# One decoder layer on one core: second and third norm folded, x1 transposed before its norm, the batch loop written out

## The chip, the cores and the metric

The kernel runs on 1 core of one Trainium2 chip. The time is the device time of one execution in microseconds (us); lower is better. The core has engines with one instruction queue each: PE (matmuls), DVE (VectorE), ACT (ScalarE), POOL (GpSimd) and SP, which only issues transfers. Each runs its queue in order; they wait for one another on semaphores.

## What is computed

Four sequences (B = 4) of T = 256 rows, D = 256 columns, in f32. Cut to what matters:

```
h  = layernorm(x);  q,k,v = h@Wq, h@Wk, h@Wv; rotary on q,k
x1 = x + rms_norm(lightning_attention(q,k,v)) @ Wo     # 16 heads of 16, chunks of 128, a decay per head
kv  = ctx @ W_k.T + b_k                                 # 256 x 64
sim = (layernorm(x1) @ kv) @ kv.T / 16                  # 256 x 256
z   = (sim - mean(sim)) * rsqrt(var(sim) + 1e-6) * gamma + beta
x2  = x1 + softmax(z)
h3  = layernorm(x2); logits = h3 @ Wr; gate = softmax of the two largest of 8
out = x2 + sum_e gate[e] * (h3 @ We[e] + be[e])
```

Note for the change that a row of softmax(z) sums to 1, so its mean is 1/256.

## The kernel before, in words

Each sequence is two tiles of 128 rows (t = 0, 1). The work of a sequence has three stages: **front** (norm 1, q/k/v, rotary, attention, x1), **back** (norm 2, context product, similarities, softmax, x2, norm 3, routing) and **experts** (8 units, u = 0 to 7; a unit is one tile times two experts, six f32r matmuls of 512 columns, a high and low part product, into one bank of 2 KB per partition). Passes are skewed: pass i does the front of sequence i, the back of sequence i-1 and the experts of sequence i-2. Pass 0 has a front only, pass 1 front and back, passes 2 and 3 all three (these two are called the full passes here), pass 4 back and experts, pass 5 experts only. Passes 2 and 3 are one hardware loop (L263).

The order on each queue is written out by hand in one `body(i, front, back, experts)` per engine. `late(steady=..., last=...)` marks where the expert work of the older sequence goes: on PE the units (`expert_unit`), on DVE the additions (`add_units(b, q)`: four additions, n = 4q to 4q+3, two for each of the units 2q and 2q+1, in the order tile 0, tile 1, tile 0, tile 1). A unit that reuses a bank waits on PE for the additions that read it (`s_exd`). Eight banks: `bank[0..5]` for everything, `ebank[0..1]` for the experts. In a full pass the units 2 and 3 go to bank2 and bank3, the others alternate between the two ebanks.

What the prediction's steps touch, in a full pass:

- PE: `qkv(t)` is the q/k product (L784, 512 columns) followed by the v product (256 columns) into `bank[2 + t]`. For t = 1 that is bank3, which also holds the similarities of tile 0, so `qkv(1)` waits for `s_z` of both tiles between its two products. Then the transposes of q and k (L961), `scores`, the transposes of x2 (L799), `attend`, `project`.
- ACT: copies out of PSUM. `normalize_similarities` (L411) writes `z` and increments `s_z`; `head_queries` (kT L423, qx L425) follows the q/k transposes, then the second `softmax_exp` (ez L417).
- DVE: norm statistics (`ln_stats`: stats L519, mv L522, ve L524), `ln_apply` (norm L530), additions (L557), `softmax_input` (zg L592, zb L594, nmax L598), `rotate` (L584, L587), `residual2` (rsum L604, x2 L606), `decay_scores` (probs L613), `route` (gates, L621 to L654), x1 (L767).
- POOL: every rsqrt as a power (L325), the addition of the experts' biases to `acc` once 12 additions are done (L336), the sine half of the rotary (rot_b L346), the decayed keys (L352).
- `keep_clock(n, bank)` (L792) issues n matmuls that nobody reads.

Of the kernel before, what the change touches and what calls it, by code (L numbers as in the profile page):

```python
# [100 lines left out]
def decoder_layer(nc, x, ctx, wq, wk, wv, wo, rms_w, w_k, b_k, ln_gamma, ln_beta, wr, we, be,  # L101
                  consts, decay, out):
    with ExitStack() as stack:
# [211 lines left out]
        def _(pool):  # L315
# [11 lines left out]
            def body(i, front, back, experts):  # L327
                if back:
                    rsqrt(rs[1], ve[1], i - 1, s_var[1], s_rstd[1])
                if front:  # L330
# [719 lines left out]
```

## Time and profile before

| | |
|---|---|
| time, median of 3 runs (lowest to highest) | 180.23 us (179.91 to 180.83) |
| profiled execution: span from first to last instruction | 178.7 us |
| profiled execution: its own time | not given apart from the span; the median lies 1.5 us above the span |
| PE busy | 152.3 us (85%) |
| DVE busy | 126.4 us (71%) |
| ACT busy | 61.8 us (35%) |
| POOL busy | 35.9 us (20%) |
| mean granted TensorE clock | 0.971 of full speed |
| DMA over the span | 7.29 MB, mean 41 GB/s |

Busy time counts instructions of an engine; PE's matmuls are pipelined and their ends are modelled. "Idle before" names the time an engine stood idle just before a row, and "<-" what ended that idle time. A granted clock of 1.00 is 2.4 GHz and 0.50 is 1.2 GHz.

### The profile page before, as it was taken

What the parts mean: (1) busy time and instruction counts of PE and PEld (TensorE: products, weight loads), DVE (VectorE), ACT (ScalarE), POOL (GpSimd) and SP (SyncE); (2) the same over time, 40 slices, a digit from 0 to 9 for tenths busy, and PEclk for the clock granted to TensorE, in tenths of its full rate; (3) what the DMA queues carried; (4) which work ended last, traced back from release to release, by engine and by line L of the source; (5) the groups of instructions that cost most, each with busy time, mean ns of one, the idle gap of its engine ahead of it and who ended that gap; (6) DMA issues with size and microseconds to landing.
All of it is one profiled execution on the core that took longest, in us unless ns stands there. A gap on an engine that the chain in (4) does not pass through costs nothing.

```text
span 178.7 us, 3036 instructions
## 1 busy us (share of the span) xinstructions
PE 152.3 (85%) x983; PEld 106.6 (60%) x983; DVE 126.4 (71%) x396; ACT 61.8 (35%) x171; POOL 35.9 (20%) x54
## 2 busy tenths in 40 slices
PE   0399964797997999999959999999599889998991
PEld 0267433573662678867626888677258757745880
DVE  0633599647487995975789959757899565877762
ACT  3346880103487132054751320547613220311110
POOL 3104163013161002222410013125100113010020
PEclk9999996569999999999999999999999999999999
DMA  5999200000200000000004000000010000001001
GB/s 173 290 360 340 57 0 4 0 0 2 69 10 0 0 4 0 0 2 0 0 4 132 0 0 0 0 0 0 0 59 0 4 2 0 0 0 59 4 0 59
DMA packets 7930, 7.29 MB, mean 41 GB/s; under 512 B 2264, under 2 KB 7664, under 8 KB 7792
## 3 DMA queue, kind: packets, MB, share of 16 engines
q1 hardware_dynamic: 7424, 6.79, 12.1%
q10 hardware_dynamic: 496, 0.37, 0.7%
q8 instruction: 6, 0.10, 0.2%
q14 instruction: 4, 0.03, 0.1%
HBM read 6.11 MB, written 1.05 MB: 40 GB/s over the span
## 4 chain that ended last, share of the span: by engine, by line
PE 43%; DVE 33%; issue 7%; ACT 6%; DVEq 5%; POOL 3%; DMA 2%; POOLq 0%
PE bank L784 15%; PE ebank L784 11%; DVE probs L613 9%; PE bank L894 4%; POOL rs L325 3%; DVE b_e_parts L738 3%; DVE stats L519 2%; ACT qx L425 2%; PE ebank L792 2%; DMA xin<-in_x 2%; DVE norm L530 2%; DVEq L520 2%; PE bank L799 2%; DVE acc L557 2%; PE bank L890 1%
## 5 line engine op out<-in xcount | busy, mean ns | idle before, releaser
L613 DVE TENSOR_TENSOR probs<-bank,dec 128x512 f32<-128x512 f32 x32 | 19.8, 683 | 1.9 <-PE bank L852 1.9
L852 PE MATMUL bank<-qx,kT 64*128 64x512 f32 x64 | 18.4, 625 | 0.7 <-ACT kv L480 0.7
L325 POOL TENSOR_TENSOR rs<-ve,nhalf 128x2 f32<-128x2 f32 x16 | 11.4, 711 | 36.6 <-DVE ve L524 36.5
L877 PE MATMUL bank<-probs,vpad 128*32 128x128 f32 x256 | 10.8, 293 | 4.1 <-DVE probs L613 4.1
L799 PE MATMUL bank<-cst,norm 128*128 128x128 f32 x36 | 6.4, 301 | 9.1 <-DVE norm L530 9.1
L784 PE MATMUL ebank<-w_e_hi,h3T_hi 128*128 128x512 f32 x40 | 13.3, 413 | 0.0
L557 DVE SCALAR_TENSOR_TENSOR acc<-ebank,gate,acc 128x256 f32<-128x256 f32 x26 | 11.3, 477 | 2.5 <-PE ebank L784 2.3
L425 ACT ACTIVATE qx<-bank,cst 128x256 f32<-128x256 f32 x32 | 12.6, 489 | 0.0
L557 DVE SCALAR_TENSOR_TENSOR acc<-bank,gate,acc 128x256 f32<-128x256 f32 x22 | 9.3, 478 | 4.5 <-PE bank L784 3.0
L784 PE MATMUL ebank<-w_e_hi,h3T_lo 128*128 128x512 f32 x40 | 12.5, 393 | 0.0
L784 PE MATMUL ebank<-w_e_lo,h3T_hi 128*128 128x512 f32 x40 | 12.4, 392 | 0.0
L346 POOL TENSOR_TENSOR rot_b<-qk,cst 128x128 f32<-128x128 f32 x16 | 7.9, 510 | 20.4 <-ACT qk L399 20.4
L799 PEld LDWEIGHTS bank<-cst,norm 128*128 128x128 f32 x36 | 4.3, 149 | 12.4 <-issue 7.9
L325 POOL TENSOR_TENSOR rms_rs<-rms_ve,nhalf 128x2 f32<-128x2 f32 x4 | 2.8, 692 | 44.0 <-DVE rms_ve L760 44.0
L393 ACT COPY pT<-bank 128x256 f32<-128x256 f32 x8 | 2.7, 376 | 25.7 <-PE bank L799 25.7
L877 PEld LDWEIGHTS bank<-probs,vpad 128*32 128x32 f32 x256 | 8.1, 115 | 5.7 <-issue 4.3
L852 PEld LDWEIGHTS bank<-qx,kT 64*128 64x128 f32 x64 | 7.4, 185 | 6.4 <-DVE probs L613 2.1
L336 POOL TENSOR_TENSOR acc<-acc,biases 128x512 f32<-128x512 f32 x4 | 5.1, 1286 | 29.5 <-DVE acc L557 29.5
L894 PE MATMUL bank<-w_o,attT 128*128 128x256 f32 x32 | 10.4, 454 | 0.0
L433 ACT ACTIVATE sqT<-bank 128x256 f32<-128x256 f32 x8 | 3.1, 385 | 21.1 <-PE bank L877 14.2
L784 PE MATMUL bank<-w_qkv_hi,h1T_hi 128*128 128x512 f32 (+1 forms) x32 | 9.6, 382 | 0.0
L792 PE MATMUL ebank<-cst 128*128 128x512 f32 x16 | 8.8, 674 | 0.0
(135 smaller groups left out, 332.8 us busy)
## 6 DMA issues: line engine op xcount, KB each, us to landing
w_e<-in_L_ffn_We SPq DMA_DIRECT2D x2, 1024.0 KB, 10.8
xin<-in_x SPq DMA_DIRECT2D x4, 256.0 KB, 3.6
dec<-in_decay SPq DMA_DIRECT2D x1, 1024.0 KB, 7.9
out<-outb SPq DMA_DIRECT2D x8, 128.0 KB, 1.7
cst<-in_consts ACTq DMA_DIRECT2D x1, 282.0 KB, 3.6
w_qkv<-in_L_attn_Wq SPq DMA_DIRECT2D x1, 256.0 KB, 4.2
w_qkv<-in_L_attn_Wk SPq DMA_DIRECT2D x1, 256.0 KB, 4.6
w_qkv<-in_L_attn_Wv SPq DMA_DIRECT2D x1, 256.0 KB, 4.9
```

The source lines that it names most:

```text
L325: nc.gpsimd.tensor_tensor(dst[:], src[:], nhalf[:], ALU.pow).then_inc(done, 1)
L346: nc.gpsimd.tensor_tensor(rot_b[:, t, :, a, :], v[:, :, 1 - a, 0:ROT], sin, ALU.mult).then_inc(s_rb, 1)
L425: o = act.activation(qx[:, t, :, k, :], bank[t][:, 0:D].rearrange("p (g n) -> p g n", g=GROUPS), ACT.Copy, scale=cst[:, C_PICK + k:C_PICK ...
L557: nc.vector.scalar_tensor_tensor(out=outb[:, t, :] if last else acc[:, t, :], in0=expert_bank(b, u)[:, (e % 2) * D:(e % 2 + 1) * D], scala ...
L613: nc.vector.tensor_tensor(probs[:, t, 4 * n:4 * n + 4, :], bank[2 + n][:].rearrange("p (h n) -> p h n", h=4), dec[:, 4 * n:4 * n + 4, :], ...
L738: nc.vector.tensor_tensor(b_e_s[64:96], b_e[64:96], b_e_s[64:96].bitcast(F32), ALU.subtract).then_inc(s_be_lo, 1)
L784: mm = pe.matmul(dst, a[ka][:, c, a_cols], b[kb][:, c, b_cols], start=(n == 0 and c == 0), stop=(n == 2 and c == KC - 1))
L792: pe.matmul(dst[:], ident, cst[:, 0:512], start=True, stop=True)
L799: mm = pe.transpose(banks[t][:, c * P:(c + 1) * P], norm[n][:, t, c * P:(c + 1) * P], ident)
L852: pe.matmul(bank[2 + n][:], kT[rows, t, g, :], qx[rows, t, g, :, :], start=True, stop=True).then_inc(s_sc_ps, 1)
L877: mm = pe.matmul(bank[t][32 * q:32 * q + 32, g * P:(g + 1) * P], vpad[:, t, h, :], probs[:, t, h, :], start=(par == 0), stop=(par == 1 and ...
L894: mm = pe.matmul(bank[2 + t][:, 0:D], attT[:, t, g, :], w_o[:, g, :], start=(g == 0), stop=(g == GROUPS - 1))
```

## The change

The second norm and the norm over the similarities are folded together. ACT centres the context keys over their 256 columns (a sum with `accum_out`, a shift, a second pass), so the rows of sim have mean zero and the product can take x1 as it is; the scale of norm 2 goes into the epsilon of the similarities' norm (`ve3 = sum of squares / 256 + 1e-6 * (var(x1) + 1e-5)`). The sum of squares is taken by ACT. x2 is kept centred (x1 minus its mean minus 1/256), so norm 3 needs only its scale, which goes into the gates (`gate_y`), into the exponent of the two-way softmax and, with the mean, into the biases. Both norms' `ln_apply`, the statistics on DVE over sim and ACT's `z` go; `s_z` is now incremented by DVE's first operation of `softmax_input`. PE transposes x1 and x2 themselves. The PE and DVE order of a full pass is rewritten, all 8 units of a full pass alternate between the two ebanks, POOL's order changes, and the loop over passes 2 and 3 is written out. The diff, cut, with its pieces in the order loop, expert banks, POOL, ACT, DVE, PE:

```diff
-            with eng.Fori(2, B) as i:
+            for i in range(2, B):
                 body(i, True, True, True)
...
-            return bank[u] if 2 <= u < (EARLY if is_last(b) else 4) else ebank[(u + 1) % 2]
+            own = EARLY if is_last(b) else 4 if isinstance(b, int) and b == B - 2 else 0
+            return bank[u] if 2 <= u < own else ebank[(u + 1) % 2]
...
-                if back:
-                    rsqrt(rs[1], ve[1], i - 1, s_var[1], s_rstd[1])
                 if front:
                     rsqrt(rs[0], ve[0], i, s_var[0], s_rstd[0])
+                if back and front:
+                    rsqrt(rs[3], ve[3], i - 1, s_sv, s_sr)
                 if experts:
                     pool.wait_ge(s_gb_sb, i - 1)
                     pool.wait_ge(s_exd, TILES * E * (i - 2) + biases_after(i - 2))
                     nc.gpsimd.tensor_tensor(acc[:], acc[:], biases[:], ALU.add).then_inc(s_acc, 1)
-                if back:
+                if back and not front:
                     rsqrt(rs[3], ve[3], i - 1, s_sv, s_sr)
...
-                def normalize_similarities(t):
-                    act.activation(z[:, t], sim_banks[t][:, 0:T], ACT.Identity, bias=sim_b[:, t:t + 1],
-                                   scale=rs[3][:, t:t + 1]).then_inc(s_z, 1)
+                def square_similarities(t):
+                    act.activation(sim_sq[:, t], sim_banks[t][:, 0:T], ACT.Square,
+                                   accum_out=ssq[:, t:t + 1]).then_inc(s_sq, 1)
+                def center_x1(t):
+                    act.activation(x1c[:, t], x1[:, t], ACT.Identity, bias=nmu3[:, t:t + 1]).then_inc(s_x1c, 1)
+                def center_context():
+                    act.activation(kvT[:], bank[5][:, 0:T], ACT.Identity, bias=b_ctx[:],
+                                   accum_out=ksum[:]).then_inc(s_ksum, 1)
+                    act.wait_ge(s_ksum, i + 1)
+                    act.activation(kshift[:], ksum[:], ACT.Identity, bias=b_ctx[:], scale=-1.0 / T).then_inc(s_kshift, 1)
+                    act.wait_ge(s_kshift, i + 1)
+                    act.activation(kvT[:], bank[5][:, 0:T], ACT.Identity, bias=kshift[:]).then_inc(s_c, 1)
...
+                    act.wait_ge(s_rstd[2], i)
+                    for t in range(TILES):
+                        o = act.activation(gexp[:, t:t + 1], gdiff[:, t:t + 1], ACT.Exp, scale=rs[2][:, t:t + 1])
...
                 def softmax_input(t):
+                    nc.vector.scalar_tensor_tensor(out=zg[:, t], in0=sim_banks[t][:, 0:T], scalar=rs[3][:, t:t + 1],
+                                                   in1=gam[:], op0=ALU.mult, op1=ALU.mult).then_inc(s_z, 1)
                     dve.wait_ge(s_z, TILES * j + t + 1)
-                    nc.vector.tensor_tensor(zg[:, t], z[:, t], gam[:], ALU.mult)
...
+                    nc.vector.tensor_tensor(gate_y[:], gate[:], rs[2][:].unsqueeze(2).to_broadcast([P, TILES, E]),
+                                            ALU.mult).then_inc(s_gate, 1)
...
                 if back:
                     dve.wait_ge(s_x1, TILES * i)
-                    ln_stats(1, lambda t: x1[:, t, :], s_var[1])
+                    ln_stats(1, x1)
+                    x1_means(j)
                 if front:
                     dve.wait_ge(s_x, 16 * (i + 1))
-                    ln_stats(0, lambda t: xin[:, t, :], s_var[0])
-                if back:
-                    ln_apply(1, x1, j)
+                    ln_stats(0, xin)
+                    ln_variance(0)
                 late(steady=0, last=0)
                 if front:
-                    ln_apply(0, xin, i)
+                    normalize_x(i)
                 late(steady=1)
-                late(steady=2)
...
                 late(last=1)
                 if back:
-                    dve.wait_ge(s_sim, i)
-                    ln_stats(3, lambda t: sim_banks[t][:, 0:T], s_sv)
+                    dve.wait_ge(s_sq, TILES * i)
+                    dve.wait_ge(s_mu3, i)
+                    nc.vector.scalar_tensor_tensor(out=ve[3][:], in0=ssq[:], scalar=1.0 / T, in1=ve[1][:],
+                                                   op0=ALU.mult, op1=ALU.add).then_inc(s_sv, 1)
+                late(steady=2, last=2)
+                if back:
                     dve.wait_ge(s_sr, i)
-                late(last=2)
-                if back:
                     softmax_input(0)
                 if front:
                     rotate(0)
...
                 late(steady=3)
-                if back:
-                    ln_apply(2, x2, j)
...
-                    elif u in (2, 3):
-                        pe.wait_ge(s_x1, TILES * (b + 1) + t + 1)
-                    elif isinstance(b, int) and b == B - 2 and u >= EARLY:
-                        pass
-                    elif u >= 4:
-                        pe.wait_ge(s_exd, TILES * E * b + (0 if u < 6 else 8) + 3 + t)
+                    elif isinstance(b, int) and b == B - 2 and u >= 2:
+                        if u < 4:
+                            pe.wait_ge(s_x1, TILES * (b + 1) + t + 1)
+                        elif u < EARLY:
+                            pe.wait_ge(s_exd, TILES * E * b + 3 + t)
+                    elif u >= 2:
+                        pe.wait_ge(s_exd, TILES * E * b + 4 * (q - 1) + 3 + t)
...
-                late(steady=(0, 1, 2, 3, 4), last=(0, 1))
+                late(steady=(0,), last=(0, 1))
                 if back:
                     transposes(1, j, bank[4:6])
-                late(steady=(5,), last=(2,))
+                late(steady=(1,), last=(2,))
...
-                late(last=(3,))
+                late(steady=(2,), last=(3,))
...
-                late(steady=(6,), last=(4, 5, 6, 7))
+                late(steady=(3, 4), last=(4, 5, 6, 7))
...
                     pe.matmul(bank[5][:, 0:T], w_ctxT[:], ctxT[:], start=True, stop=True).then_inc(s_c_ps, 1)
+                    late(steady=(5,))
                     qkv(1)
+                    late(steady=(6,))
```

`pkvT` also takes the opposite sign, and `nbet` (minus beta, made once by ACT in pass 0) with a minimum in place of the maximum spares the two `nmax` operations.

How the order on the queues moves, for a full pass. First PE, from the v product of `qkv(0)` to the v product of `qkv(1)`; bank3 is the v bank of tile 1, bank5 the context's, ebank0 the bank of unit 5. Before:

```order
L784 MATMUL bank2<-w_qkv_lo,h1T_hi 128x256 x2
L954 MATMUL bank5<-ctxT,w_ctxT 128x256
L784 MATMUL bank1<-w_qkv_hi,h1T_hi 128x512 [waits ln1_T_low_part]
L784 MATMUL bank1<-w_qkv_lo,h1T_hi 128x512 x2
L784 MATMUL bank3<-w_qkv_hi,h1T_hi 128x256 [waits sim_normalized]
```

Now:

```order
L823 MATMUL bank2<-w_qkv_lo,h1T_hi 128x256 x2
L990 MATMUL bank5<-ctxT,w_ctxT 128x256
L823 MATMUL ebank0<-w_e_hi,h3T_hi 128x512 [waits expert_products_added]
L823 MATMUL ebank0<-w_e_lo,h3T_hi 128x512 x2
L823 MATMUL bank1<-w_qkv_hi,h1T_hi 128x512 [waits ln1_T_low_part]
L823 MATMUL bank1<-w_qkv_lo,h1T_hi 128x512 x2
L823 MATMUL bank3<-w_qkv_hi,h1T_hi 128x256 [waits sim_scaled]
```

Unit 5 now stands directly ahead of `qkv(1)`, and the semaphore that the v product of tile 1 waits for is incremented by DVE's zg of both tiles (L632), no longer by ACT's z.

Second DVE and POOL at the same place. DVE now, from the last row of norm 1's low parts to zg of tile 1:

```order
L579 TENSOR_TENSOR h1T_lo<-bank1,h1T_hi 128x2x128 [waits ln1_T_on_sbuf]
L733 SCALAR_TENSOR_TENSOR ve3<-ssq,ve1 128x2 [waits x1_mean,sim_squares]
L598 SCALAR_TENSOR_TENSOR acc<-ebank1,gate_y,acc 128x256 [waits expert_products_added,expert_pair_in_psum]
L598 SCALAR_TENSOR_TENSOR acc<-ebank0,gate_y,acc 128x256 [waits expert_products_added,expert_pair_in_psum]
L632 SCALAR_TENSOR_TENSOR zg<-bank3,rs3,gam 128x256 [waits sim_rstd]
L625 TENSOR_TENSOR rot_a<-qk,cst 128x256 [waits qk_on_sbuf]
L628 TENSOR_TENSOR qk<-rot_a,rot_b 128x64x4 [waits rotary_cross_terms,vector_front_step]
L632 SCALAR_TENSOR_TENSOR zg<-bank4,rs3,gam 128x256
```

and POOL now, from the start of the pass:

```order
L334 TENSOR_TENSOR rs0<-ve0,nhalf 128x2 [waits ln1_variance]
L334 TENSOR_TENSOR rs3<-ve3,nhalf 128x2 [waits sim_variance]
L345 TENSOR_TENSOR acc<-acc,biases 128x512 [waits expert_products_added,expert_bias_on_sbuf]
L355 TENSOR_TENSOR rot_b<-qk,cst 128x32x4 [waits qk_on_sbuf]
L355 TENSOR_TENSOR rot_b<-qk,cst 128x32x4
```

The four additions of the units 4 and 5 (two rows of each bank) moved on DVE from ahead of h1T_lo to behind it and ahead of zg; POOL's addition of the biases keeps its place ahead of rot_b.

Third PE at the start of a full pass, now:

```order
L823 MATMUL ebank1<-w_e_lo,h3T_hi 128x512 x2
L839 MATMUL bank4<-cst,x1 128x128 [waits x1_ready]
L823 MATMUL ebank0<-w_e_hi,h3T_hi 128x512 [waits logits_read]
L957 MATMUL bank2<-pT,kv 64x128 [waits ln2_T_on_sbuf,context_step_on_sbuf]
L823 MATMUL ebank1<-w_e_hi,h3T_hi 128x512 [waits expert_products_added]
L839 MATMUL bank0<-cst,norm 128x128 [waits ln1_normalized,ctx_loaded,expert_bias_on_sbuf]
L967 MATMUL bank5<-cst,cin 64x128 x2
L976 MATMUL bank3<-kvT,pkvT 128x256 [waits pkv_on_sbuf]
L823 MATMUL ebank0<-w_e_hi,h3T_hi 128x512 [waits expert_products_added]
L823 MATMUL ebank1<-w_e_hi,h3T_hi 128x512 [waits expert_products_added]
```

Before, the units 0 to 4 stood in one run ahead of the x1 transposes, units 2 and 3 in bank2 and bank3 waiting only for x1; now unit 2 takes ebank1 again and waits for the additions of unit 0, and unit 4 follows unit 3 directly and waits for those of unit 2.

## Rows read from the trace of the kernel before

**Rows 1.** busy us per pass: PE, PEld, DVE, ACT, POOL; clock; DMA

```profile
39.00:69.20 30.20, 27.06 (x201) 17.26 (x201) 22.52 (x81) 13.04 (x39) 6.24 (x10) 1.00 0.04 12
69.20:105.10 35.90, 32.95 (x239) 24.49 (x238) 28.84 (x98) 13.49 (x40) 7.41 (x11) 1.00 0.05 17
...
141.00:163.50 22.50, 21.27 (x92) 13.56 (x91) 16.28 (x52) 4.49 (x12) 3.38 (x4) 1.00 0.04 12
```

**Rows 2.** timeline of PE, pass 3: start, us, instruction, idle before it

```profile
104.96 0.62 PE L784 MATMUL ebank<-w_e_hi,h3T_hi 128*128 128x512 f32 x2
...
113.69 0.60 PE L799 MATMUL bank<-cst,norm 128*128 128x128 f32 x4
...
117.48 0.63 PE L784 MATMUL bank<-w_qkv_hi,h1T_hi 128*128 128x512 f32 x2
...
118.88 0.40 PE L784 MATMUL bank<-w_qkv_hi,h1T_hi 128*128 128x256 f32 x2
...
122.52 0.60 PE L961 MATMUL bank<-cst,qk 128*128 128x128 f32 x4
...
129.84 0.67 PE L799 MATMUL ebank<-cst,norm 128*128 128x128 f32 x4 [1.53 <-DVE norm L530]
```

**Rows 3.** timeline of DVE, pass 3

```profile
108.98 0.87 DVE L557 SCALAR_TENSOR_TENSOR acc<-ebank,gate,x 128x256 f32<-128x256 f32 x2
...
113.98 1.27 DVE L557 SCALAR_TENSOR_TENSOR acc<-ebank,gate,acc 128x256 f32<-128x256 f32 x3 [0.74 <-PE ebank L784]
...
121.48 0.42 DVE L587 TENSOR_TENSOR qk<-rot_a,rot_b 128x256 f32<-128x256 f32 x1 [0.65 <-POOL rot_b L346]
...
125.57 0.16 DVE L604 RECIPROCAL rsum<-esum 128x1 f32<-128x1 f32 x1 [0.34 <-ACT ez L417]
...
129.29 0.73 DVE L530 TENSOR_SCALAR norm<-x,mv,rs 128x256 f32<-128x256 f32 x2
129.93 2.48 DVE L613 TENSOR_TENSOR probs<-bank,dec 128x512 f32<-128x512 f32 x4
...
138.34 0.17 DVE L648 TENSOR_TENSOR gate<-gpart 128x16 f32<-128x16 f32 x1
138.54 0.17 DVE L651 CAST gate_parts<-gate 128x16 fp32r<-128x16 f32 x1
```

**Rows 4.** timeline of ACT, pass 3

```profile
118.42 1.02 ACT L411 ACTIVATE z<-bank,sim_b,rs 128x256 f32<-128x256 f32 x2 [2.29 <-DVE sim_b L696]
```

**Rows 5.** timeline of POOL, pass 3

```profile
115.32 1.28 POOL L336 TENSOR_TENSOR acc<-acc,biases 128x512 f32<-128x512 f32 x1 [6.04 <-DVE acc L557]
...
120.45 1.00 POOL L346 TENSOR_TENSOR rot_b<-qk,cst 128x128 f32<-128x128 f32 x2 [2.26 <-ACT qk L399]
```

**Rows 6.** timeline of POOL, pass 0

```profile
23.68 4.53 POOL L360 TENSOR_TENSOR w_e_lo<-w_e,w_e_hi 128x2048 fp32r<-128x2048 f32 x1 [5.15 <-ACT w_e_hi L490]
```

**Rows 7.** timeline of DVE, pass 0, beside Rows 6

```profile
23.86 4.62 DVE L738 TENSOR_TENSOR b_e_parts<-b_e,b_e_parts 32x256 fp32r<-32x256 f32 x1
```

**Rows 8.** timeline of PE, pass 1

```profile
51.46 0.63 PE L961 MATMUL bank<-cst,qk 128*128 128x128 f32 x4 [0.35 <-DVE qk L587]
```

**Rows 9.** timeline of DVE, pass 1

```profile
57.34 0.74 DVE L530 TENSOR_SCALAR norm<-x,mv,rs 128x256 f32<-128x256 f32 x2 [0.81 <-POOL rs L325]
```

**Rows 10.** timeline of PE, pass 4

```profile
144.41 0.76 PE L799 MATMUL bank<-cst,norm 128*128 128x128 f32 x4 [0.54 <-DVE norm L530]
...
154.93 5.31 PE L792 MATMUL bank<-cst 128*128 128x512 f32 x12
...
162.55 0.36 PE L991 MATMUL bank<-w_r_hi_lo,h3T_hi 128*128 128x16 f32 x2 [0.69 <-DVE h3T_lo L538]
```

**Rows 11.** timeline of PE, pass 0, idle before it

```profile
29.44 1.36 PE L877 MATMUL bank<-probs,vpad 128*32 128x128 f32 x14 [4.08 <-DVE probs L613]
```

**Rows 12.** granted clock, pass 0, columns as in Rows 1

```profile
27.00:29.00 2.00, 0.00 (x0) 0.00 (x0) 1.97 (x3) 0.00 (x0) 1.21 (x1) 0.81 0.00 0
...
37.00:39.00 2.00, 2.00 (x8) 1.77 (x8) 0.64 (x2) 0.00 (x0) 0.70 (x1) 0.63 0.00 0
```

More of the change, by code:

```diff
@@ L145, in decoder_layer @@
         rs = [sb(f"rs{n}", [P, TILES]) for n in range(4)]
-        norm = [sb(f"norm{n}", [P, TILES, D]) for n in range(3)]
+        norm = sb("norm", [P, TILES, D])
         h1T = [sb(f"h1T_{n}", [P, KC, T], F32R) for n in ("hi", "lo")]
@@ L165, in decoder_layer @@
         pkvT = sb("pkvT", [TILES * DC, P])
-        sim_b = sb("sim_b", [P, TILES])
-        z = sb("z", [P, TILES, T])
+        mu3 = [sb(f"mu3_{n}", [P, TILES]) for n in range(2)]
+        nmu3 = sb("nmu3", [P, TILES])
+        x1c = sb("x1c", [P, TILES, D])
+        sim_sq = sb("sim_sq", [P, TILES, T])
+        ssq = sb("ssq", [P, TILES])
         zg = sb("zg", [P, TILES, T])
         zb = sb("zb", [P, TILES, T])
-        zmax = sb("zmax", [P, TILES])
         nmax = sb("nmax", [P, TILES])
@@ L187, in decoder_layer @@
         gate = sb("gate", [P, TILES, E])
+        gate_y = sb("gate_y", [P, TILES, E])
         gate_s = sb("gate_parts", [P, TILES, P], F32R)
@@ L363, in body @@
                     rsqrt(rms_rs, rms_ve, i, s_rms_var, s_rms_rstd, TILES)
-            passes(pool, body)
+            passes(body)
         @block.scalar
@@ L437, in body @@
                     transposed(1, j, bank[4:6], pT)
+                if back:
+                    act.wait_ge(s_pk_ps, i)
+                    act.activation(pkvT[:], pkv_bank[:, 0:P], ACT.Copy, scale=-SIM_SCALE).then_inc(s_pk, 1)
+                    act.wait_ge(s_mu3, i)
+                    center_x1(0)
                 if front and not back:
@@ L506, in body @@
                         act.wait_ge(s_acc, i - 1)
-                    act.copy(biases[:], bank[1][:].rearrange("p (t n) -> p t n", t=TILES)).then_inc(s_gb_sb, 1)
-            passes(act, body)
+                    for t in range(TILES):
+                        o = act.activation(biases[:, t], bank[1][:, t * D:(t + 1) * D], ACT.Identity, bias=mu3[j % 2][:, t:t + 1])
+                    o.then_inc(s_gb_sb, 1)
+            passes(body)
         @block.vector
@@ L559, in add_units @@
                         in0=expert_bank(b, u)[:, (e % 2) * D:(e % 2 + 1) * D],
-                        scalar=gate[:, t, e:e + 1], in1=acc[:, t, :] if e else x2[:, t, :],
+                        scalar=gate_y[:, t, e:e + 1], in1=acc[:, t, :] if e else x2[:, t, :],
                         op0=ALU.mult, op1=ALU.add).then_inc(s_exd, 1)
@@ L770, in body @@
                 assert (not front or vf.n == vf.each) and (not back or vb.n == vb.each), (vf.n, vb.n)
-            passes(dve, body)
+            passes(body)
         @block.tensor
@@ L794, in transposes @@
             def transposes(n, b, banks):
+                src, ready = ((norm, s_norm), (x1, s_x1), (x2, s_x2))[n]
                 for t in range(TILES):
-                    pe.wait_ge(s_norm[n], TILES * b + t + 1)
+                    pe.wait_ge(ready, TILES * b + t + 1)
                     for c in range(KC):
-                        mm = pe.transpose(banks[t][:, c * P:(c + 1) * P], norm[n][:, t, c * P:(c + 1) * P], ident)
+                        mm = pe.transpose(banks[t][:, c * P:(c + 1) * P], src[:, t, c * P:(c + 1) * P], ident)
                     mm.then_inc(s_nT_ps[n], 1)
@@ L1023, in body @@
                         expert_unit(j, u)
-            passes(pe, body)
+            passes(body)
 _INS = ["x", "ctx_512", "L0_attn_Wq", "L0_attn_Wk", "L0_attn_Wv", "L0_attn_Wo", "L0_attn_rms_w",
```

99 lines of the change are left out of this document (51 added, 48 removed).

## The prediction

> **What bounds the kernel now.** I read the busy time per pass first, then the chain of waits to see which engine carries each stretch, then the timelines of one full pass engine by engine. By passes the time is 30.2 us for pass 1, 35.9 for each full pass (2 and 3) and 22.5 for pass 4 [rows 1]; pass 0 takes the 39 ahead of them and pass 5 the 15 behind. In a full pass PE is busy 33.0 of 35.9 us and DVE 28.8, so PE has under 3 us to give away and DVE 7. The timelines show where each is the bound. PE starts pass 3 at 104.96 with expert unit 0 and runs without a gap to the q/k transposes at 122.52; its first long gap, 1.53 us, comes at 129.84, where it waits for the third norm [rows 2]. From there DVE sets the pace: it waited for the second softmax exponential at 125.57 (which on ACT stands behind the head queries of tile 0, which follow the transposes of 122.52), and from then on it works through x2, its statistics, the last four additions, the norm, 8 decays and the routing without stopping until 139 [rows 3]. So the first half of a full pass is PE's order, the second half is DVE's, and the hinge is the transpose of q/k at 122.52: what makes it late makes the pass late, one for one.
>
> **What the change removes.** It takes both norm operations of x1 and x2, the statistics over sim, z and nmax: some 3 us of DVE work per pass. Most of it lies in DVE's slack of the first half. What lies on the path:
> - Full pass: the norm of x2, 129.29 to 129.93 [rows 3], 0.65 us each.
> - Pass 1: there is no addition between the statistics and the norm, so DVE also waits for POOL's power: see there.
> - Pass 4: x2's norm hides behind `keep_clock`, see below.
>
> **What it adds, small.** gate_y is one more waited step in the routing, behind which gate_parts, project and the next pass stand: gate to its successor is 0.20 us [rows 3], in passes 1, 2, 3. Centring the keys, the squares and x1c are some eight ACT operations of 0.2 to 0.5 us; ACT is busy 13.5 of 35.9 us and none falls between the head queries and the exponential, so 0 (if ACT were late, qkv(0)'s v product in pass 1 would wait some 0.5 us for ctxT, which the longer wait below swallows). The written-out loop: pass 3 starts at 104.96 with no idle time before it [rows 2], so there is no branch stall to win, 0. The Trainium skill (Runtime: NRT & Kernel Launch, Instruction fetch mechanics) says that a taken branch can break the prefetch of instructions and stall; by it the loop's end would be worth something, by the row it is worth nothing, and the sum takes nothing.
>
> **What it moves: three waits on PE, in each full pass.**
>
> (a) Unit 2 goes back to ebank1 and needs unit 0's third addition. The stretch 104.96 to 113.69 holds six units and the x1 transposes [rows 2], 8.73 us: about 1.4 for a unit and 0.4 for the transposes. The stretch 113.69 to 117.48 holds one unit and four small groups, so some 0.6 each, the context product among them. PE reaches unit 2 after two units, transposes and context product: 3.8 us into the pass. DVE's first addition was at 108.98 [rows 3]; without the x1 norm (0.65) and with two more small steps (0.16) it is at 108.5, 3.5 us in. Additions follow each other every 0.40 and one lasts 0.48 (three in 1.27), so the third ends at 4.8. Wait: 1.0 us.
>
> (b) Unit 4 directly follows unit 3 and needs the third of the additions of units 2 and 3; the second of them needs unit 3 itself. From PE's end of a unit to the addition that waited for it: 113.69 to 113.98 [rows 2, 3], 0.29. Then 0.40 + 0.48 + 0.05. Wait: 1.2 us. Before, the banks of the other units spared this.
>
> (c) The v product of `qkv(1)` waits for zg of both tiles. Before, ACT's z was done at 119.44 [rows 4] and PE wanted it for the last product ahead of 122.52, at some 121.8: no wait. Now zg of tile 1 stands on DVE behind: the additions of unit 5 (which PE finishes only just ahead of `qkv(1)`), zg of tile 0, and `rotate(0)`, which needs POOL's rot_b, which stands on POOL behind the addition of the biases, which needs the 12th addition. From unit 5's end: 0.29, three additions 1.27, semaphore 0.08, POOL's biases 1.28 and rot_b 1.00 [rows 5], rotate 0.37 (0.42 for the row [rows 3], less overlap), zg 0.48 (as the additions, same form), 0.05: 4.8 us. In that time PE has the q/k product, 117.48 to 118.88 = 1.40 [rows 2]. Wait: 3.4 us. DVE's own part (zg, zb, rot_a, 1.4 us) fits beside POOL's 2.3.
>
> (d) In (c) DVE's zb and rot_a, with two operands in SBUF, now run beside POOL. In pass 0 such a step of 32x256 lasted 4.62 us beside a POOL step of 4.53 and ended 0.27 after it [rows 6, 7], where 128x256 otherwise takes 0.42. Bounds: 0, if POOL's chain covers it, to 0.3 per pass, if rot_a ends 0.27 behind rot_b; I take 0.1, since DVE has 0.9 of slack there. The Trainium skill (SBUF — State Buffer, SBUF: two separate sides) says the port is an exclusive lock for the whole instruction and that the one who comes second fully blocks; the pass 0 rows agree. If POOL were also held up by DVE, as that rule allows, the sum would be some 0.5 per pass longer than mine.
>
> The units ahead of the q/k transposes number seven before and now, so these waits delay the hinge by 1.0 + 1.2 + 3.4 = 5.6. DVE's slack does not absorb it: it is the consumer. Behind the hinge nothing else changes. One full pass: 5.6 - 0.65 + 0.2 + 0.1 = +5.25; two: **+10.5**.
>
> Pass 1 has the wait (c) without units and biases. qkv(0) starts some 0.5 earlier there, and from its end I count copy 0.5, rot_b 1.0, rotate 0.4, zg 0.5, v product 0.7 to the q/k transposes: 51.4, where they start now at 51.46 after 0.35 of waiting [rows 8]; so it costs 0. The gain is the norm's slot and the wait for POOL ahead of it, 0.65 + 0.81 = 1.45 [rows 9], less 0.2: **-1.25**. Pass 4: PE issues 12 clock matmuls, 5.31 us from 154.93 on, however early x2 is, and logits start at 162.55, after 0.69 of waiting for h3T_lo, which DVE did behind the last four additions [rows 10]. x1's transposes waited 0.54 for the norm at 144.41, which goes; with small savings behind it the clock matmuls start 0.7 to 1.0 earlier. x2 is ready well ahead of their end (about 156: no statistics of sim, no z, no nmax), so DVE does the last additions before x2's transposes arrive, not between them and h3T_lo, and the 0.69 goes too. 0.9 + 0.7: **-1.6**, logits at 160.9. Passes 0 and 5: 0 (in pass 5 PE is dense to the end; the later biases have 1.5 us of room).
>
> **Sum.** -1.25 + 10.5 - 1.6 = +7.65 on the profiled span of 178.7, so 186.35; the median of the runs is 180.23, 1.5 above the span, so the forecast is **187.9 us**.
>
> **The rivals.**
> 1. *The clock falls in gap (c).* In pass 0 PE stood idle 4.08 us [rows 11], and the granted clock had fallen to 0.50 before it resumed and was back only in the stretch 37 to 39 [rows 12]; from 0.81 as the mean of 27 to 29 the fall came about 2.9 us into the gap. A gap of 3.4 us with little before it could do the same, while 1.53 us did not. Then v product and unit 6, 2.1 us, run at 1.2 GHz ahead of the hinge: +2.1 per pass, 187.9 + 4.2 = 192.1 if both passes fall. For it: the length. Against: PE is dense on both sides. The Trainium skill (TensorE: Matmul & The Clock Gate, HAM oscillation) warns that idle gaps between matmuls can return the array to the half clock; the rows of pass 0 agree.
> 2. *The other side: faster.* The mechanism is DVE slack. DVE stands idle 7.1 us in a full pass [rows 1]; if the pass were set by its work and the 5.6 us of PE's waits went into that idle time, only the removals would count: 2 x (-0.65 + 0.2) - 1.25 - 1.6 = -3.75, 176.5 us. It decides if the q/k transposes come no later than now. For it: 3 us less DVE work per pass. Against: at 125.57 DVE waits for ez with 0.34 idle [rows 3], so its second half cannot begin before the hinge.
> 3. *Only (c) is real.* If the additions keep up, so that (a) and (b) vanish, the sum is 4.4 less: 183.5. If instead (c) were short and the early waits balanced the gains, the change would measure as none, near 180.
>
> **Chances.** Forecast 0.73, rival 1 0.12, rival 3 0.05 (183.5), rival 2 0.07, no change 0.03. A measurement of this kernel can tell about 0.5% from no change. So faster 0.07, same 0.03, slower 0.90. The range must leave out 2 in 10: it goes from 183.5 (rival 3) to 191.5, which takes in the upper end of (d), a clock that falls in one pass or somewhat less than 4.2 in all, and leaves out rivals 2 and the worst of 1.
>
> **What would show it.** In the changed kernel's timeline: in both full passes PE idle 1.0 ahead of the third unit and 1.2 ahead of the fifth, released by DVE's additions; 3.4 us between q/k and v product of tile 1, released by zg; POOL's rot_b starting right behind its biases; full passes of 41.1 us, pass 1 of 29, pass 4 of 21; third-norm gap gone. Right on the total and wrong on the mechanism would be: full passes long but the gap elsewhere. I am wrong if `rot_b` starts before the biases' addition ends, if the granted clock falls below 1.00 after pass 0, or if the full passes are not longer than 36 us.

## The result and the profile after

The changed kernel takes **190.27 us** (median of four runs, 188.78 to 190.56) against 180.5 us (179.91 to 180.83): 1.053 times the time before, 95% interval 1.048 to 1.057. The forecast was 187.9 with a range of 183.5 to 191.5. In the experiments below, a run more than 1.5% above the fastest run of its kernel is left out of the median.

The profiled execution has a span of 188.5 us against 178.7, so 9.8 us are to be found. Busy time by pass of the changed kernel, to be compared with [rows 1] (stretch and its length, busy PE, PEld, DVE, ACT, POOL, granted clock, DMA share, GB/s):

```profile
38.60:67.50 28.90, 26.69 (x204) 17.35 (x203) 20.09 (x74) 14.40 (x47) 5.35 (x10) 1.00 0.04 13
67.50:109.60 42.10, 34.77 (x241) 25.24 (x240) 27.23 (x90) 15.41 (x49) 6.69 (x10) 0.96 0.05 15
109.60:152.40 42.80, 34.84 (x241) 25.52 (x240) 27.26 (x90) 15.41 (x49) 6.69 (x10) 0.96 0.02 7
152.40:173.20 20.80, 20.80 (x92) 13.85 (x92) 14.83 (x43) 5.25 (x17) 2.68 (x3) 1.00 0.04 13
```

Pass 1 became shorter, both full passes longer by over 6 us, pass 4 shorter. Boundaries taken from PE's timeline: 1.5 us less up to pass 2 (unit 0 at 67.47, before 69.01), 42.10 for pass 2 (before 35.95, **+6.15**), 42.78 for pass 3 (before 35.99, **+6.79**), 19.79 to the logits (before 21.60, -1.81), +0.21 behind them. That is the whole 9.8.

PE's timeline, changed kernel, pass 2 (start, us, instruction, idle ahead of it and who ended it):

```profile
67.47 0.62 PE L823 MATMUL ebank<-w_e_hi,h3T_hi 128*128 128x512 f32 x2
...
72.28 0.73 PE L823 MATMUL ebank<-w_e_hi,h3T_hi 128*128 128x512 f32 x2 [0.82 <-DVE acc L598]
...
77.79 0.73 PE L823 MATMUL ebank<-w_e_hi,h3T_hi 128*128 128x512 f32 x2 [0.97 <-DVE acc L598]
...
88.55 0.50 PE L823 MATMUL bank<-w_qkv_hi,h1T_hi 128*128 128x256 f32 x2 [3.36 <-DVE zg L632]
...
89.36 0.63 PE L823 MATMUL ebank<-w_e_hi,h3T_hi 128*128 128x512 f32 x2
89.83 0.97 PE L823 MATMUL ebank<-w_e_hi,h3T_lo 128*128 128x512 f32 x2
90.60 1.05 PE L823 MATMUL ebank<-w_e_lo,h3T_hi 128*128 128x512 f32 x2
91.45 1.05 PE L999 MATMUL bank<-cst,qk 128*128 128x128 f32 x4
```

Here are the three waits at the three places: 0.82 ahead of the third unit, 0.97 ahead of the fifth, 3.36 ahead of the v product of tile 1. Pass 3 shows them again with the same numbers. Measured as a delay (the distance to the start of the row ahead, less the same distance where nothing waits), they are 0.90, 1.13 and 3.53, together 5.56, where the forecast had 5.6. The duration column says more: unit 6, 89.36 to 91.45, takes 2.09 where a unit takes 1.40 (2.48 in pass 3, 131.92 to 134.40), and its pieces last 0.97 and 1.05 instead of 0.63. The clock says why.

Granted clock in 2 us stretches of passes 2 and 3, changed kernel (columns as above):

```profile
86.00:88.00 2.00, 0.00 (x0) 0.00 (x0) 1.64 (x4) 0.60 (x2) 1.57 (x3) 1.00 0.00 0
88.00:90.00 2.00, 1.45 (x9) 1.36 (x10) 1.49 (x6) 0.43 (x1) 0.00 (x0) 0.98 0.02 4
90.00:92.00 2.00, 2.00 (x7) 1.50 (x7) 1.10 (x2) 0.15 (x1) 1.58 (x3) 0.50 0.03 8
92.00:94.00 2.00, 2.00 (x9) 1.40 (x8) 0.09 (x1) 1.46 (x5) 0.00 (x0) 0.67 0.00 0
...
130.00:132.00 2.00, 1.35 (x7) 1.35 (x8) 1.59 (x6) 0.00 (x0) 0.00 (x0) 0.72 0.00 0
132.00:134.00 2.00, 2.00 (x6) 1.57 (x6) 0.51 (x2) 0.59 (x1) 1.18 (x3) 0.50 0.02 4
```

In the gap nothing ran on PE (0.00 busy); in the stretch behind it, the granted clock is 0.50, the lower of its two levels (1.2 GHz), and on its way back at 92 to 94; the next stretch of each pass has 1.00 (94 to 96) and 0.93 (134 to 136). In pass 3 it is lower already for the v product. This is rival 1, at a smaller price.

One of the forecast's signs did not come. The gap ahead of the transposes of x2 is still there, in both full passes (1.22 here and 1.50 in pass 3; before 1.57 and 1.53); PE now waits for the last additions in place of the norm:

```profile
98.63 0.66 PE L839 MATMUL ebank<-cst,x 128*128 128x128 f32 x4 [1.22 <-DVE outb L598]
```

The other engines in the same gap. DVE, changed kernel, pass 2:

```profile
83.83 1.27 DVE L598 SCALAR_TENSOR_TENSOR acc<-ebank,gate_y,acc 128x256 f32<-128x256 f32 x3 [3.85 <-PE ebank L823]
85.01 0.47 DVE L632 SCALAR_TENSOR_TENSOR zg<-bank,rs,gam 128x256 f32<-128x256 f32 x1
85.52 1.26 DVE L635 CUSTOM_DVE_ANT_0 zb<-zg,nbet 128x256 f32<-128x256 f32 x1
...
86.71 0.61 DVE L625 TENSOR_TENSOR rot_a<-qk,cst 128x256 f32<-128x256 f32 x1
87.68 0.42 DVE L628 TENSOR_TENSOR qk<-rot_a,rot_b 128x256 f32<-128x256 f32 x1 [0.36 <-POOL rot_b L355]
88.02 0.48 DVE L632 SCALAR_TENSOR_TENSOR zg<-bank,rs,gam 128x256 f32<-128x256 f32 x1
```

and POOL, the same stretch:

```profile
85.24 1.26 POOL L345 TENSOR_TENSOR acc<-acc,biases 128x512 f32<-128x512 f32 x1 [5.61 <-DVE acc L598]
86.46 1.12 POOL L355 TENSOR_TENSOR rot_b<-qk,cst 128x128 f32<-128x128 f32 x2
```

POOL does what was forecast: rot_b directly behind the biases. But zb on DVE lasts 1.26 us, where it lasts 0.42 elsewhere, and it ends at 86.78, 0.28 behind the addition of the biases on POOL (86.50). In pass 0 it was 0.27 [rows 6, 7].

In pass 1, PE (the v product waits 0.46 for zg; then the q/k transposes):

```profile
50.57 0.51 PE L823 MATMUL bank<-w_qkv_hi,h1T_hi 128*128 128x256 f32 x2 [0.46 <-DVE zg L632]
...
51.39 0.60 PE L999 MATMUL bank<-cst,qk 128*128 128x128 f32 x4
```

In pass 4, PE, and DVE's x2 of tile 1:

```profile
165.60 5.31 PE L831 MATMUL bank<-cst 128*128 128x512 f32 x12
170.75 0.60 PE L839 MATMUL bank<-cst,x 128*128 128x128 f32 x4
...
172.14 0.36 PE L1029 MATMUL bank<-w_r_hi_lo,h3T_hi 128*128 128x16 f32 x2
```

```profile
166.85 0.48 DVE L645 SCALAR_TENSOR_TENSOR x<-ez,rsum,x1c 128x256 f32<-128x256 f32 x1
```

x2 was ready at 167.3; its transposes stand behind six clock matmuls, as before [rows 10], and the wait of 0.69 for h3T_lo is gone.

### The profile page after: what moved, and what is told of

The parts are those of the page before. It is cut to its first block, busy times and chain, and to the rows that moved or that the text cites. A ratio compares the mean times of both kernels' runs of the same rounds, so it can differ in the third digit from the quotient of the medians.

```text
span 188.5 us, 2833 instructions
## 1 busy us (share of the span) xinstructions
PE 154.7 (82%) x983; PEld 108.2 (57%) x983; DVE 119.0 (63%) x364; ACT 69.4 (37%) x208; POOL 32.9 (17%) x50
## 3 DMA queue, kind: packets, MB, share of 16 engines
q1 hardware_dynamic: 7424, 6.79, 11.6%
HBM read 6.11 MB, written 1.05 MB: 38 GB/s over the span
## 4 chain that ended last, share of the span: by engine, by line
PE 48%; DVE 31%; issue 6%; ACT 4%; POOL 4%; DVEq 3%; DMA 2%; POOLq 0%
PE ebank L823 15%; PE bank L823 14%; DVE probs L652 9%; PE bank L935 3%; PE bank L831 3%; DVE acc L598 3%; DVE b_e_parts L777 2%; ACT qx L447 2%; DMA xin<-in_x 2%; DVE stats L551 2%; PE ebank L831 2%; PE bank L839 2%; DVEq L552 2%; POOL rot_b L355 2%; PE bank L931 1%
## 5 line engine op out<-in xcount | busy, mean ns | idle before, releaser
L598 DVE SCALAR_TENSOR_TENSOR acc<-ebank,gate_y,acc 128x256 f32<-128x256 f32 x34 | 14.9, 478 | 16.6 <-PE ebank L823 16.5
L823 PE MATMUL ebank<-w_e_hi,h3T_hi 128*128 128x512 f32 x48 | 17.1, 438 | 3.6 <-DVE acc L598 3.6
L334 POOL TENSOR_TENSOR rs<-ve,nhalf 128x2 f32<-128x2 f32 x12 | 8.3, 695 | 52.2 <-DVE ve L559 34.6
L823 PE MATMUL ebank<-w_e_hi,h3T_lo 128*128 128x512 f32 x48 | 15.8, 413 | 0.0
L823 PE MATMUL ebank<-w_e_lo,h3T_hi 128*128 128x512 f32 x48 | 15.8, 412 | 0.0
L823 PEld LDWEIGHTS bank<-w_qkv_hi,h1T_hi 128*128 128x128 f32 x32 | 5.7, 196 | 11.7 <-DVE zg L632 8.5
L823 PEld LDWEIGHTS ebank<-w_e_hi,h3T_hi 128*128 128x128 f32 x48 | 8.0, 199 | 7.2 <-DVE acc L598 5.3
L408 ACT COPY qk<-bank 128x512 f32<-128x512 f32 x8 | 4.7, 586 | 18.1 <-PE bank L823 18.1
L823 PEld LDWEIGHTS ebank<-w_e_lo,h3T_hi 128*128 128x128 f32 x48 | 9.6, 200 | 2.4
L823 PEld LDWEIGHTS ebank<-w_e_hi,h3T_lo 128*128 128x128 f32 x48 | 9.3, 194 | 2.3
```

The costliest lines, as they stand in the source:

```text
L334: nc.gpsimd.tensor_tensor(dst[:], src[:], nhalf[:], ALU.pow).then_inc(done, 1)
L408: act.copy(qk[:, t, :], bank[t][:]).then_inc(s_qk, 1)
L598: nc.vector.scalar_tensor_tensor(out=outb[:, t, :] if last else acc[:, t, :], in0=expert_bank(b, u)[:, (e % 2) * D:(e % 2 + 1) * D], scala ...
L823: mm = pe.matmul(dst, a[ka][:, c, a_cols], b[kb][:, c, b_cols], start=(n == 0 and c == 0), stop=(n == 2 and c == KC - 1))
```

## The experiments

The theory: the loss is the three waits in the full passes, above all the one for zg of tile 1, and the half clock that this wait causes; the folded arithmetic itself is a gain. The rival: the fold, with its added ACT steps and its steps beside POOL, or the written-out loop, carries a part.

**The loop alone**

```diff
-            with eng.Fori(2, B) as i:
+            for i in range(2, B):
```

> The kernel before with its loop over passes 2 and 3 written out, nothing else. My theory (the change's loss is its new waits on PE; the loop's branch costs nothing): 180.2, within 0.5 of before. Rival (the folded arithmetic or the written-out loop carries part of the difference): slower by 1 or more, or faster by 1 if the branch stalled an engine.

Measured 180.76 us, ratio 1.0019 (0.9992 to 1.0045), span 178.1. The loop is worth nothing here, as the sum had it.

**rot_b of tile 0 ahead of the biases, on POOL** (`cross(0)` is the loop's body for tile 0)

```diff
+                if front and experts:
+                    cross(0)
                 if experts:
...
                     nc.gpsimd.tensor_tensor(acc[:], acc[:], biases[:], ALU.add)
```

> The changed kernel with POOL's rot_b of tile 0 ahead of the addition of the biases in passes 2 and 3. If the v product of tile 1 waits 3.36 us because rot_b stands behind the biases on POOL (as I predicted): the wait falls by 1.3 to 2.1 in each pass and the total by 2.6 to 5. If it is zb on DVE, which lasts 1.26 us beside the addition of the biases, that holds zg of tile 1 back, only the 0.36 ahead of the rotation goes: 0.7 in all, 189.5, and zb still lasts 1.2.

Measured 188.62 us (186.55 to 189.28), 1.65 less, which is no more than the changed kernel's own runs differ by. The wait tells more; it fell only from 3.36 to 2.85 (2.84 in pass 3):

```profile
88.99 0.50 PE L830 MATMUL bank<-w_qkv_hi,h1T_hi 128*128 128x256 f32 x2 [2.85 <-DVE zg L639]
```

DVE in that stretch:

```profile
86.47 1.26 DVE L642 CUSTOM_DVE_ANT_0 zb<-zg,nbet 128x256 f32<-128x256 f32 x1
...
88.11 0.42 DVE L635 TENSOR_TENSOR qk<-rot_a,rot_b 128x256 f32<-128x256 f32 x1
```

rot_b was long done, and DVE never waited for it; zb still lasts 1.26. So two chains, 0.36 us apart, stood between unit 5 and zg of tile 1, POOL's queue and DVE's zb held up by POOL, and taking one away gives 0.5 of 3.36. The forecast's 3.4 was right in size with only one of the two chains in its working. The clock fell here too, and in pass 3 before PE resumed (columns as above):

```profile
130.00:132.00 2.00, 1.00 (x4) 1.00 (x5) 1.90 (x7) 0.39 (x2) 0.00 (x0) 0.61 0.00 0
```

PE resumed at 131.00. Half a clock from there on alone would give a mean of 0.75; 0.61 puts the fall at 130.4.

**The biases at the 8th addition**

```diff
-            return 8 if isinstance(b, int) and b >= B - 2 else 12
+            return 8
```

> The changed kernel with POOL adding the biases behind the 8th addition instead of the 12th in passes 2 and 3 (as in pass 4 already), so that this step of 1.26 us lies beside no step between unit 5 and zg of tile 1. With rot_b alone taken from behind it the wait for zg went from 3.36 to 2.85 and zb still lasted 1.26. If the biases' addition holds DVE's zb up: zb back at 0.42, rot_a at 0.42, wait for zg 3.36 - 0.84 - 0.36 - 0.19 = 2.0; two passes 2.8 less and, if the clock stays full over 2.0 us, another 2.8: 184.7 to 187.5. If zb is slow by itself in this place: 189, as with rot_b moved.

Measured 186.0 us (185.44 to 186.79), 4.3 less. The wait is 2.01 in both passes, where 2.0 was expected, because zb is back at 0.42:

```profile
84.26 0.42 DVE L635 CUSTOM_DVE_ANT_0 zb<-zg,nbet 128x256 f32<-128x256 f32 x1
```

PE's v product and the clock, pass 2 (84 to 90) and pass 3 (124 to 130) of this kernel:

```profile
85.94 0.51 PE L823 MATMUL bank<-w_qkv_hi,h1T_hi 128*128 128x256 f32 x2 [2.01 <-DVE zg L632]
```

```profile
86.00:88.00 2.00, 2.00 (x12) 1.78 (x13) 1.34 (x5) 0.59 (x1) 0.38 (x1) 1.00 0.05 12
...
126.00:128.00 2.00, 2.00 (x8) 1.76 (x8) 0.88 (x3) 0.58 (x1) 0.34 (x1) 0.50 0.01 4
```

After the same gap of 2.01 us the clock stays full in pass 2 (39.57 us long) and falls in pass 3 (41.41). The length of a gap alone does not decide it.

**Both zg ahead of zb and the rotation** (`scale_gamma` is zg's step taken out of `softmax_input`, which keeps zb)

```diff
+                    scale_gamma(0)
+                    scale_gamma(1)
                     softmax_input(0)
```

> The changed kernel with zg of both tiles ahead of zb and the rotation of tile 0 on DVE. My theory (the v product waits for zg of tile 1, and the gap lets the clock fall): wait of 1.2 in place of 3.36 in each pass, granted clock full in passes 2 and 3, the q/k transposes no later for the rotation: 2 x 2.15 and 2.8 for the clock, 7.1 less, 183.2. Rival (banks or folded arithmetic are the cost, the v product only waits where something else would): no more than 1 less, 189.

Measured **181.7 us** (181.24 to 182.24), 8.6 less than the changed kernel: one step of DVE, zg of tile 1, moved ahead of three others (zb, rot_a and their sum with rot_b) brings the time to within 1.2 us of the kernel before. 183.2 was expected, with a wait of 1.2. Wait 0.74, granted clock 1.00 from pass 1 on, full passes 38.50 and 38.77 us:

```profile
84.22 0.51 PE L828 MATMUL bank<-w_qkv_hi,h1T_hi 128*128 128x256 f32 x2 [0.74 <-DVE zg L632]
```

Between the two profiled executions (9.3 us), the full passes give 7.6 (42.10 + 42.78 - 38.50 - 38.77) and pass 1 0.3. The other 1.4 lies in pass 0, which this edit does not touch: its end, the start of the clock matmuls of pass 1, lies between 37.4 and 39.1 in the kernels of this study (39.05 in the changed one, 37.66 here). So the move itself is worth 7.6 of the 12.9 us that the full passes had lost, some 2.7 of it the clock, as the filled gap below shows. DVE and POOL, the same stretch:

```profile
83.30 0.87 DVE L632 SCALAR_TENSOR_TENSOR zg<-bank,rs,gam 128x256 f32<-128x256 f32 x2
84.08 1.00 DVE L638 CUSTOM_DVE_ANT_0 zb<-zg,nbet 128x256 f32<-128x256 f32 x1
```

```profile
83.52 1.27 POOL L345 TENSOR_TENSOR acc<-acc,biases 128x512 f32<-128x512 f32 x1 [5.59 <-DVE acc L598]
```

The two zg, with one operand in PSUM, take 0.87 beside POOL's step as elsewhere; zb, with both in SBUF, takes 1.00 and ends 0.29 behind it.

**The gap filled, zg where it was**

```diff
                     elif back:
+                        if experts:
+                            pe.wait_ge(s_qk, TILES * i + 1)
+                            keep_clock(3, bank[0])
                         pe.wait_ge(s_z, TILES * i)
```

> The changed kernel with three matmuls of 128x512 (some 2.65 us, results unused) ahead of the v product's wait for zg in passes 2 and 3: the wait for zg's data stays, the idle time of PE goes. If the fallen clock is a cost of its own: granted clock full in passes 2 and 3, unit 6 at 1.40 in place of 2.09 and 2.48, the q/k transposes at 0.53: 2.8 less, 187.5. If the clock costs nothing because DVE sets the pace there: 190.3, same as the changed kernel.

Measured 187.31 us (187.14 to 187.59): **3.0 less**, with more work on PE. The wait for the data is the same (2.74 of filler and 0.80 of idle), only the clock is not:

```profile
84.69 2.74 PE L831 MATMUL bank<-cst 128*128 128x512 f32 x6
88.23 0.51 PE L823 MATMUL bank<-w_qkv_hi,h1T_hi 128*128 128x256 f32 x2 [0.80 <-DVE zg L632]
...
90.44 0.60 PE L1002 MATMUL bank<-cst,qk 128*128 128x128 f32 x4
```

Full passes: 40.97 and 41.22 us, so the clock cost 1.13 in pass 2 and 1.56 in pass 3. Note the runs too: these lie within 0.45 us, those of the changed kernel within 1.8. The shortest of those, 188.78, has a mean granted clock of 0.973, the other three 0.955; that the clock makes the spread is likely, not shown.

**The folded arithmetic in the order of before.** Units 0 to 4 first, unit 5 behind x1's transposes, the banks and waits of before, additions 0 to 11 early, the biases ahead of rstd of sim on POOL, h1T ahead of pkvT on ACT, both zg first.

```diff
-                late(steady=(0,), last=(0, 1))
+                late(steady=(0, 1, 2, 3, 4), last=(0, 1))
...
-                late(steady=(3, 4), last=(4, 5, 6, 7))
+                late(steady=(6,), last=(4, 5, 6, 7))
...
-                    late(steady=(5,))
                     qkv(1)
-                    late(steady=(6,))
```

> The folded arithmetic in the order of the kernel before: units 0 to 4 first, the banks of before, additions 0 to 11 early, the biases ahead of the rstd of sim on POOL, zg of both tiles first. My theory (the loss is the three waits and the clock, the fold itself is worth 0.5 per full pass, 1.7 in pass 1 and 1.8 in pass 4): 180.3 - 1.0 - 1.7 - 1.8 = 175.8. Rival (the fold puts as much on ACT and on the steps beside POOL as it takes from DVE): 179 to 181.

Measured **176.13 us** (176.07 to 176.21), ratio 0.977 (0.974 to 0.980). Same arithmetic as the changed kernel, 14.1 us less: the order, with the banks and waits that belong to it, is the whole loss, and the fold is a gain of 2.3%. By pass (unit 0 to unit 0 or logits):

```profile
66.80:102.30 35.50, 32.99 (x240) 24.43 (x239) 26.09 (x90) 15.26 (x49) 6.62 (x10) 1.00 0.07 18
102.30:138.00 35.70, 32.92 (x241) 24.47 (x240) 26.18 (x90) 15.26 (x49) 6.62 (x10) 1.00 0.03 9
138.00:157.80 19.80, 19.80 (x85) 12.83 (x83) 14.51 (x43) 5.14 (x17) 2.67 (x3) 1.00 0.04 13
```

and PE, q/k transposes and the next unit 0 in pass 3:

```profile
119.99 0.60 PE L1006 MATMUL bank<-cst,qk 128*128 128x128 f32 x4
...
137.99 0.62 PE L828 MATMUL ebank<-w_e_hi,h3T_hi 128*128 128x512 f32 x2
```

35.55 and 35.66 us in the full passes (before 35.95 and 35.99), so the fold is worth 0.4 there; 28.79 against 30.18 in pass 1, 19.80 against 21.60 in pass 4. Against both zg first in the new order, the full passes are 2.95 and 3.11 shorter; the three waits left there (0.81, 0.97 and 0.74, none of them here) are 2.5 of it. The waits (a) and (b) were not taken away one by one.

**Three clock matmuls in pass 4 instead of six**, on the changed kernel and on the last one:

```diff
-                    keep_clock(6, bank[2])
+                    keep_clock(3, bank[2])
```

> The changed kernel with 3 instead of 6 clock matmuls of 512 columns in pass 4 (2.65 us less). x2 was ready at 167.3 there and the clock matmuls ran to 170.7. If they are what makes x2's transposes late: 2.65 less, 187.6. If the additions or h3T_lo are behind them just as late, or the clock falls: within 1 of 190.3.

> Both: the folded arithmetic in the old order and 3 clock matmuls in pass 4: the sum of the two, 175.8 - 2.65 = 173.2 by my theory; 178 if each is worth only half.

On the changed kernel two runs measured 187.84 and 188.29 us (mean granted clock 0.972) and two 190.95 and 191.14 us (0.946), where the changed kernel itself has 188.78 to 190.56. The two shorter ones are 0.7 below its shortest run, the two longer ones above its longest: these runs don't settle whether anything was gained. On the folded arithmetic in the old order it is 175.28 us (174.85 to 175.76), 0.85 less than 176.13. 2.65 was expected. In the second kernel's trace:

```profile
151.37 2.74 PE L836 MATMUL bank<-cst 128*128 128x512 f32 x6
...
156.53 0.36 PE L1036 MATMUL bank<-w_r_hi_lo,h3T_hi 128*128 128x16 f32 x2 [1.12 <-DVE h3T_lo L578]
```

The additions into outb and h3T_lo on DVE are next: PE waits 1.12 for them, and of 2.57 us of clock matmuls only 1.4 is won (pass 4 is 18.40 long, before that 19.80). In the first kernel's trace, of the 191.14 us run, 1.4 is won in pass 4 as well (18.42 against 19.79), but the wait of 1.14 is followed by a granted clock of 0.50 (173 to 175); from the logits to unit 4 of the last sequence it takes 8.55 there and 7.02 in the second. There the whole saving was paid back to the clock.

**Two further edits.** The exponential of tile 1 ahead of ACT's head queries, with x2 of tile 1 ahead of the sum of rotate(1); and, in pass 4, the statistics of x2 behind h3T_lo.

```diff
                     queries_keys(1)
-                    head_queries(0)
                 if back:
                     softmax_exp(1)
+                if front:
+                    head_queries(0)
```

```diff
                 if back:
                     low_parts(2, j, ln3_banks, h3T)
+                if back and not front:
+                    ln_stats(2, x2)
+                    ln_variance(2)
```

> The folded arithmetic in the old order with 3 clock matmuls in pass 4 (175.3), and ACT's second exponential ahead of head_queries of tile 0, with x2 of tile 1 on DVE ahead of the sum of rotate(1), in the 0.72 us where DVE waits for rot_b. If DVE's second half of a full pass is what sets its end and the exponential is what starts it: the statistics of x2 begin 0.8 to 1.0 earlier in each full pass, 173.5. If the head queries, 0.6 later, make scores(0) late and that sets the end: 175.3 or slower.

> The same version (175.3) with the statistics of x2 in pass 4 behind h3T_lo instead of ahead of the last additions. In its trace DVE works from 149.96 to 156.7 with 0.32 idle, and PE waits 1.12 for h3T_lo. If DVE's order is the tail's path: the logits come 1.2 earlier and the routing, which then stands behind the statistics, 0.7: 174.6. If POOL's power of the variance becomes late: no gain, 175.3.

> Both of the former edits: they lie in different passes, so their gains should add: 175.3 - 1.8 - 0.7 = 172.8. If either gain is taken up behind it: 173.5 to 175.

Measured, in this order, 174.11 us (173.46 to 174.41), 173.73 us (173.51 to 174.61) and **171.42 us** (171.35 to 172.58), the last at ratio 0.953 (0.947 to 0.958). The first won 1.1 and 0.9 in the full passes (34.43 and 34.72 long against 35.55 and 35.65), as expected, but lost 1.6 in the tail (17.95 behind the logits against 16.37): behind the 1.13 of waiting for h3T_lo the clock fell this time. Clock in the tail of that first kernel, columns as above:

```profile
154.00:156.00 2.00, 2.00 (x13) 1.80 (x14) 1.00 (x9) 0.24 (x2) 0.00 (x0) 0.95 0.38 125
156.00:158.00 2.00, 2.00 (x6) 1.55 (x5) 1.73 (x15) 0.24 (x2) 0.00 (x0) 0.50 0.02 4
```

The second edit alone brings the logits 1.2 us earlier in pass 4 (17.22 against 18.40), as expected. In the combined version it has taken the wait for h3T_lo away, and the tail has a granted clock of 1.00:

```profile
151.96 1.02 PE L850 MATMUL bank<-cst 128*128 128x512 f32 x2
152.92 0.36 PE L1050 MATMUL bank<-w_r_hi_lo,h3T_hi 128*128 128x16 f32 x2
```

So together they gave 3.9 (175.28 to 171.42), more than the 1.2 and 1.55 of each alone, since the 1.6 that the first alone lost to the clock did not arise. This version beats both kernels: 5% less than before.

## Why the prediction was right, and where it was not

- **(a), (b), (c): right.** 1.0, 1.2 and 3.4 were forecast, 0.90, 1.13 and 3.53 came. With the gap filled, so that the clock stays up, the full passes are 5.02 and 5.23 longer than before, where the sum had 5.25, and the kernel takes 187.31 us against the forecast's 187.9. Reading the interval from an addition to the next, and from a unit to its first addition, from [rows 2, 3] was enough.
- **(c), the chain behind it: half wrong.** The forecast called POOL's biases and rot_b the path and said that DVE's part fits beside them. DVE's part was only 0.36 shorter than POOL's (its wait for rot_b at 87.68), where the forecast had 0.9, because zb took 1.26.
- **(d): mis-sized.** 0.1 with bounds 0 and 0.3 was taken. zb was held up by 0.84 and rot_a by 0.19. It cost the pass little only because POOL's chain covered it; without that cover it cost 0.84 (biases at 8 against rot_b moved: 2.85 to 2.01). The row of pass 0 [rows 6, 7] pointed to it: the step on DVE ended 0.27 behind POOL's. By that row zb, begun 0.28 behind a POOL step of 1.26, was to be put at the rest of POOL's step (0.98) and 0.27, not at 0.42. The Trainium skill (SBUF — State Buffer, SBUF: two separate sides) says that the second to come fully blocks; zb's end 0.28 behind POOL's step agrees.
- **x2's norm and gate_y: right in size.** From the q/k transposes to the next unit 0 it is 18.00 with the fold in the old order (119.99 to 137.99), before 18.43 (122.52 to 140.95): -0.43, forecast -0.45. The sign "third-norm gap gone" was wrong: PE still waits 1.22 and 1.50 there, now for the last additions on DVE.
- **Pass 1: -1.76 (and 0.22 more in pass 0); forecast -1.25.** The q/k transposes came at 51.39 where 51.4 was forecast, partly by luck: pass 1 started 0.22 later than before, and its first half was 0.29 shorter where the forecast had no gain. Behind them it is 1.47; gate_y costs some 0.1, not 0.2.
- **Pass 4: -1.81, forecast -1.6.** Right, and for the reason given: the clock matmuls start 0.73 earlier, and the stretch behind them is 1.08 shorter, 0.69 of it the wait for h3T_lo.
- **ACT, loop: 0, right.** The loop alone measured 1.0019; the fold in the old order reached 176.13 where 175.8 was expected with nothing for ACT.
- **Rival 1 is what failed: chance and price.** It got 0.12 and came true in both passes of the profiled execution; a granted clock below 1.00 after pass 0 was one of the forecast's own signs of being wrong. The chance was argued down by "PE is dense on both sides"; the 7 us of dense PE ahead of the gap (77.79 to 85) did not keep the clock. The price was 2.1 a pass, all of v product and unit 6 at half speed; measured 1.13 and 1.56, since the fallen clock did not cover v product and unit 6 whole: by the means of 0.98 and 0.72 it fell 1.4 us after PE had resumed in pass 2 and 0.2 us after in pass 3, and in pass 3 the last piece of unit 6 (0.94) was already faster than the two ahead of it (1.05). With it the sum is 186.35 + 2.7 = 189.05 on the span, measured 188.5: without it the forecast was 2.15 short on the span (2.4 on the median), with it 0.55 long. The time lies inside the range because its upper end allowed for part of this price. The Trainium skill (TensorE: Matmul & The Clock Gate, HAM oscillation) warns that idle gaps between matmuls can bring the half clock back; the runs agree, with 0.50 behind gaps of 3.36, 2.85 and 2.01 us.
- Rivals 2 and 3 did not come: DVE is the consumer of the hinge, and all three waits are real.

## What to carry over

Where a result in PSUM moves from an early reader (ACT's copy) to a late one (a step in DVE's queue), whoever needs the bank next waits for everything ahead of that step in the queue; place the step that frees the bank first and do its consumers afterwards. Here moving that one step ahead of three others on DVE was worth 7.6 us in two passes. Judge new arithmetic and new order apart: run the new arithmetic in the old order before believing that it does not pay, and for a new idle gap on PE, carry the matmuls behind it at half speed as a case of their own with a real chance, not only the gap.

## What the runs showed of the hardware, unexpected

- Behind a gap, the clock can fall after PE has resumed: 1.00 in 86 to 88 with PE idle, 0.98 in 88 to 90, 0.50 in 90 to 92 (pass 2 of the changed kernel). It can also fall inside the gap: some 0.6 us before PE resumed with rot_b moved (pass 3, gap of 2.84), and in pass 0 of the kernel before [rows 11, 12].
- The same gap has both outcomes: 2.01 us in passes 2 and 3 of one kernel (clock 1.00 and 0.50), 1.12 and 1.13 us in the tail of two kernels (1.00 and 0.50). With the 3.36 us gap filled by 2.74 us of matmuls whose results nobody uses, it stayed at 1.00 in both passes, and the kernel was 3.0 us faster with more work.
- In these traces a step on DVE with both operands in SBUF that began behind POOL's addition of the biases ended no sooner than that addition: 1.26 for 0.42 (zb), and 1.20 for 0.15 on two columns (ve of sim in pass 4). Two zg, which read PSUM, kept their 0.87 beside the same POOL step.
